# Expert gate by tanh in two vector operations, score banks in groups of three and two, and one shared bank with six turns for each expert tile

## The reference

```python
xn = layernorm(x)
# attention: 16 heads of width 8
q, k, v = (proj(xn, W) * mod for W in (Wq, Wk, Wv))
scores = einsum('bhid,bhjd->bhij', q, k) / sqrt(8) * cos_mat
w = softmax(scores); w = (w + roll(w, 1, axis=-1)) / sqrt(2)
attn = einsum('bhij,bhjd->bhid', w, v) -> (tokens, 128) @ Wo
# experts: 8, two chosen for each token by a small attention over the expert logits
for e in range(8):
    a, g = split(x_rep @ w1[e].T, 2, axis=-1)      # 352 + 352 columns
    he = silu(a) * g @ w2[e].T                     # silu(a) = a / (1 + exp(-a))
out = x + attn + sum over the two chosen experts of score * he
```

## Time and profile before

| | us |
|---|---|
| median of 3 runs (lowest to highest) | 792.3 (790.2 to 797.7) |
| the profiled execution | 797.84 |
| its span, first to last instruction | 796.0 |

### The profile page before, as it was taken

How to read it: one execution, slowest core, us unless ns; L and a number is a source line. 1 busy time by engine, 2 the same in 40 slices (tenths; PEclk the granted TensorE clock), 3 DMA queues, 4 the chain that set the end, 5 groups by cost and what they waited for, 6 DMA issues and landing times.

```text
span 796.0 us, 11999 instructions
## 1 busy us (share of the span) xinstructions
PE 673.1 (85%) x4346; PEld 232.9 (29%) x4346; DVE 367.9 (46%) x648; ACT 534.4 (67%) x535; POOL 77.7 (10%) x91
## 2 busy tenths in 40 slices
PE   3946899798888978887988988987888899999996
PEld 1432132233323323333333333333333111111113
DVE  6652552143466366554464565555646232404002
ACT  2553968766656566655556566566665899999992
POOL 4000077200000000000000000000000245300000
PEclk9965999988989899978899799799999999999998
DMA  8346421441212112121121121121110112000001
GB/s 253 125 149 150 130 77 51 148 137 61 85 68 68 70 54 81 70 74 62 70 65 70 70 75 62 70 86 49 70 38 7 47 37 65 25 1 2 2 1 55
DMA packets 49582, 57.34 MB, mean 72 GB/s; under 512 B 7356, under 2 KB 39126, under 8 KB 49266
## 3 DMA queue, kind: packets, MB, share of 16 engines
q1 hardware_dynamic: 46546, 52.34, 20.5%
q0 software_dynamic: 2048, 4.20, 1.7%
q10 hardware_dynamic: 928, 0.00, 0.1%
HBM read 21.14 MB, written 13.63 MB: 44 GB/s over the span
## 4 chain that ended last, share of the span: by engine, by line
PE 48%; DVE 23%; ACT 12%; issue 11%; SPq 2%; DMA 2%; ACTq 1%; DVEq 0%
PE ps L1165 17%; DVE cs L823 12%; PE ps L1148 11%; ACT big L618 9%; PE ps L1082 5%; PE ps L1091 5%; PE ps L1183 3%; DVE cs L825 3%; DVE cs L828 3%; DVE m L871 2%; ACT cs L611 2%; DVE cs L822 2%; PE ps L986 2%; PE ps L1072 1%; PE ps L1025 1%
## 5 line engine op out<-in xcount | busy, mean ns | idle before, releaser
L618 ACT ACTIVATE big<-ps 128x1024 f32<-128x1024 f32 (+1 forms) x459 | 491.4, 1125 | 217.5 <-PE ps L1148 215.4
L1165 PE MATMUL ps<-big,vh 128*32 128x512 f32 x2048 | 291.8, 644 | 0.4 <-ACT big L618 0.4
L1148 PE MATMUL ps<-qa,ka 49*128 49x512 f16 x896 | 176.2, 404 | 16.6 <-DMA qa<-shift_rows 8.3
L871 DVE TENSOR_REDUCE m<-ps 128x1 f32<-128x512 f32 x128 | 88.4, 690 | 95.3 <-PE ps L1183 95.3
L823 DVE RECIPROCAL cs<-cs 128x384 f32<-128x384 f32 x39 | 99.6, 2553 | 1.4
L1148 PEld LDWEIGHTS ps<-qa,ka 49*128 49x128 f16 x896 | 38.8, 94 | 173.0 <-ACT big L618 101.1
L1091 PE MATMUL ps<-store,cs 128*128 128x128 f32 (+1 forms) x234 | 38.4, 303 | 58.1 <-DVE cs L828 58.0
L1082 PE MATMUL ps<-xgT,store 128*128 128x128 f32 (+1 forms) x468 | 80.0, 312 | 2.7 <-DMA store<-w2T 2.7
L1082 PEld LDWEIGHTS ps<-xgT,store 128*128 128x128 f32 (+1 forms) x468 | 62.1, 199 | 54.7 <-issue 51.7
L1165 PEld LDWEIGHTS ps<-big,vh 128*32 128x32 f32 x2048 | 41.2, 110 | 92.2 <-issue 81.1
L1183 PE MATMUL ps<-ka,attnT 49*128 49x512 f16 x128 | 51.5, 402 | 11.1 <-DVE m L871 11.1
(11 more groups left out here) (160 smaller groups left out, 333.3 us busy)
## 6 DMA issues: line engine op xcount, KB each, us to landing
store<-w1T SPq DMA_DIRECT2D x39, 352.0 KB, 2.6
store<-w2T SPq DMA_DIRECT2D x39, 192.0 KB, 2.5
qk_parts<-store SPq DMA_DIRECT2D x16, 256.0 KB
qa<-qk_parts SPq DMA_DIRECT2D x28, 128.0 KB
slots_x<-vh SPq DMA_DIRECT2D x5, 512.0 KB, 6.4
cs<-slots_x SPq DMA_DIRECT2D x20, 128.0 KB, 2.3
slots_y<-y SPq DMA_DIRECT2D x19, 128.0 KB, 1.8
ka<-qk_parts SPq DMA_DIRECT2D x32, 64.0 KB, 2.0
```

The lines of the kernel that those rows point to most:

```text
L618: nc.scalar.activation(probs[:, prob_of(tiles[0]):prob_of(tiles[-1]) + 1, :], ps[:, bank_of(tiles[0]):bank_of(tiles[-1]) + 1, :], ACT.Exp, ...
L871: nc.vector.tensor_reduce(m4[:, j // NC, j % NC:j % NC + 1], ps[:, O_BANKS[(p - 1) % 2], :], AX, ALU.max).then_inc(m_reduced, 1)
L1148: ins = nc.tensor.matmul(ps[:, bank_of(n), :], k[at:at + KQ, P * o:P * o + P], q[at:at + KQ, CW * c:CW * c + CW], start=True, stop=True, t ...
L1165: ins = nc.tensor.matmul(ps[32 * c:32 * c + 32, O_BANKS[p % 2], :], vh[:, p % 2, o + 8 * b, :], probs[:, prob_of(n), :], start=k == 0, sto ...
```

## The change

- The gate uses silu(a) = 0.5 a (1 + tanh(a / 2)). ScalarE computes tanh(a / 2) with the function Tanh. VectorE then does two `scalar_tensor_tensor` operations with PSUM: (t + 1) times a (`take_a`), and 0.5 times that times g (`take_g`). The add, the clamp and the reciprocal are gone.
- All 1024 score tiles go in groups of three and two in turns, over a ring of five banks (0 to 4) and fifteen SBUF slots: 410 groups.
- Bank 5 (`SIDE_BANK`) is shared by the weight transposes, the rows, a, g and the result. So g is made after a has been taken (`a_taken`), the next rows after the result has been copied (`y_copied`), and each weight block after the copy of the one before.
- An expert tile takes six turns: rows in 0, a in 1 (with the tanh), g in 3, result in 5. Expert turns run from 56 to 289. VectorE's share of a piece comes at the start of the next turn (`take_a` at the start of step 3's turn), ahead of the max job and the head's work.
- Max jobs start from the fifth quad of a head instead of the seventh, are allowed in every turn, and choose the row half that differs from the half of the group's last score tile.
- SP issues the first rows and staged weights at turn 50 (before: 66), the result store one turn later in a tile; the gather starts at quad 188 (before: 174).

```diff
+LARGE_GROUP, SMALL_GROUP = 3, 2
+RING = LARGE_GROUP + SMALL_GROUP
+PROBS = 3 * RING
+SIDE_BANK = 5
-JOB_QUAD = 6
+JOB_QUAD = 4
-EXPERTS_AT = 70
-TURNS_A_TILE = 7
-GATHER_AT = 174
+EXPERTS_AT = 56
+TURNS_A_TILE = 6
+GATHER_AT = 188
...
         def first_of(g):
-            if g < PAIRS:
-                return 2 * g
-            return min(PAIRED + GROUP_OF * (g - PAIRS), SCORE_TILES)
+            return min(RING * (g // 2) + LARGE_GROUP * (g % 2), SCORE_TILES)
...
-                if (w % QUADS >= JOB_QUAD and j < jobs_before(w // QUADS + 1) and step not in (4, 5)
-                        and (g < PAIRS or (g - j) % 2 == 0)):
-                    job = (w // QUADS, j)
+                if w % QUADS >= JOB_QUAD and j < jobs_before(w // QUADS + 1):
+                    half = (first_of(g) + 1) % 2
...
-                nc.scalar.activation(decay[:, m % 2, :], ps[:, 4, 0:FP], ACT.Exp, scale=-1.0).then_inc(decay_ready, 1)
+                nc.scalar.activation(turned_gate[:, m % 2, :], ps[:, SIDE_BANK, 0:FP], ACT.Tanh, scale=0.5).then_inc(gate_ready, 1)
...
-            def hidden(m):
+            def take_a(m):
                 k = m % 2
-                dve.wait_ge(decay_ready, m + 1)
-                then(nc.vector.tensor_scalar(decay[:, k, :], decay[:, k, :], 1.0, BIGGEST, ALU.add, ALU.min))
-                then(nc.vector.reciprocal(decay[:, k, :], decay[:, k, :]))
+                dve.wait_ge(gate_ready, m + 1)
                 dve.wait_ge(a_ready, m + 1)
-                then(nc.vector.tensor_tensor(decay[:, k, :], decay[:, k, :], ps[:, 4, 0:FP], ALU.mult))
+                nc.vector.scalar_tensor_tensor(turned_gate[:, k, :], turned_gate[:, k, :], 1.0, ps[:, SIDE_BANK, 0:FP],
+                                               ALU.add, ALU.mult).then_inc(a_taken, 1)
+
+            def take_g(m):
+                k = m % 2
                 dve.wait_ge(g_ready, m + 1)
+                dve.wait_ge(a_taken, m + 1)
                 after(dve, y_ready, m - 1)
-                nc.vector.tensor_tensor(hidT[:, k, :, :].rearrange("p f s -> p (f s)"), decay[:, k, :], ps[:, 5, 0:FP],
-                                        ALU.mult).then_inc(hidT_ready, 1)
+                nc.vector.scalar_tensor_tensor(hidT[:, k, :, :].rearrange("p f s -> p (f s)"), turned_gate[:, k, :], 0.5,
+                                               ps[:, SIDE_BANK, 0:FP], ALU.mult, ALU.mult).then_inc(hidT_ready, 1)
...
             for g, job, quads in turns():
+                m, step = expert_step(g)
+                before_m, before_step = expert_step(g - 1)
+                if weight_block(g - 1) is not None:
+                    take_weights(weight_block(g - 1))
+                if before_step == 0:
+                    rows_out(before_m)
+                if step == 3:
+                    take_a(m)
+                if before_step == 3:
+                    take_g(before_m)
+                if before_step == 5:
+                    result_out(before_m)
                 if job is not None:
                     take_max(*job)
...
-                after(pe, wT_ready, i - 1)
+                after(pe, wT_ready, i)
...
+                after(pe, y_copied, m)
+                nc.tensor.transpose(ps[:, SIDE_BANK, FP:FP + P], xg[:, m % 4, :], ident[:]).then_inc(xgT_ps, 1)
...
                 if b == 1:
-                    after(pe, y_copied, m)
+                    pe.wait_ge(a_taken, m + 1)
...
-                after(pe, exp_done, g if g == PAIRS else g - 1)
-                if g == PAIRS:
-                    pe.wait_ge(hidT_ready, TILES)
-                    pe.wait_ge(y_copied, TILES)
+                after(pe, exp_done, g - 1)
```

More of the change, by code:

```diff
@@ L240, in build @@
         xg_ld, y_wr = ([sem(f"{n}{half}") for half in range(2)] for n in ("xg_ld", "y_wr"))
-        xgT_ps, xgT_ready, a_ready, g_ready, decay_ready = (
-            sem(n) for n in ("xgT_ps", "xgT_ready", "a_ready", "g_ready", "decay_ready"))
+        xgT_ps, xgT_ready, a_ready, g_ready, gate_ready, a_taken = (
+            sem(n) for n in ("xgT_ps", "xgT_ready", "a_ready", "g_ready", "gate_ready", "a_taken"))
         hidT_ready, y_ready, y_copied, gather_ld, y_added = (
@@ L301, in groups_for, with job_in @@
         def groups_for(n):
-            if n <= PAIRED:
-                return -(-n // 2)
-            return PAIRS + -(-(n - PAIRED) // GROUP_OF)
+            whole, rest = divmod(n, RING)
+            return 2 * whole + -(-rest // LARGE_GROUP)
         def quads_for(n):
             return (n - 1) // NC + 1
-        def job_at(j):
-            return j // PER_HEAD, j // NC % NT, (2, 0, 3, 1)[j % NC]
+        def job_in(half, k):
+            r, i, c = k // (2 * NT), k // 2 % NT, 2 * half + k % 2
+            return r, i, c
         def jobs_before(p):
@@ L329, in turns @@
         def turns():
-            w, j = 0, 0
+            w, j, taken = 0, 0, [0, 0]
             for g in range(SCORE_GROUPS + 2):
-                m, step = expert_step(g)
                 job = None
-                if (w % QUADS >= JOB_QUAD and j < jobs_before(w // QUADS + 1) and step not in (4, 5)
-                        and (g < PAIRS or (g - j) % 2 == 0)):
-                    job = (w // QUADS, j)
+                if w % QUADS >= JOB_QUAD and j < jobs_before(w // QUADS + 1):
+                    half = (first_of(g) + 1) % 2
+                    if taken[half] == JOBS // 2:
+                        half = 1 - half
+                    job = (w // QUADS, j, *job_in(half, taken[half]))
+                    taken[half] += 1
                     j += 1
@@ L468, in _ @@
                     load_rows(m // 2 + 2)
-                if step == 0 and m % 2 == 0 and m >= 2:
+                if step == 1 and m % 2 == 0 and m >= 2:
                     store_results(m // 2 - 1)
-                if g == EXPERTS_AT + TURNS_A_TILE * TILES:
+                if g == EXPERTS_AT + TURNS_A_TILE * TILES + 1:
                     store_results(ROW_PAIRS - 1)
@@ L616, in weights @@
                 act.wait_ge(score_ready, g + 1)
-                after(act, pv_done, quads_for(held_before(tiles[-1]) + 1))
+                if tiles[-1] >= PROBS:
+                    act.wait_ge(pv_done, quads_for(tiles[-1] - PROBS + 1))
                 nc.scalar.activation(probs[:, prob_of(tiles[0]):prob_of(tiles[-1]) + 1, :],
@@ L636, in _ @@
                 m, step = expert_step(g)
-                if step == 3:
-                    decay_of(m)
+                if step == 1:
+                    gate_of(m)
             project(0)
@@ L805, in take_weights @@
                 dve.wait_ge(tr_ready, i + 1)
-                e, b, bank = i // NF, i % NF, 4 + i % 2
+                e, b, bank = i // NF, i % NF, SIDE_BANK
                 if b < 2:
@@ L1098, in expert_work @@
                     turn_rows(m)
-                elif step == 2:
+                elif step == 1:
                     widen(m, 0, a_ready)
@@ L1102, in expert_work @@
                     widen(m, 1, g_ready)
-                elif step == 6:
+                elif step == 5:
                     result(m)
```

47 lines of the change are left out of this document (13 added, 34 removed).

## The result

| | before | changed |
|---|---|---|
| median time, us | 792.8 (790.2 to 797.7, 4 runs) | 707.2 (706.6 to 708.3, 4 runs) |
| ratio, 95% interval | | 0.8915 [0.887, 0.896] |
| profiled execution, us | 797.8 | 706.55 |
| its span, us | 796.0 | 704.7 |
| mean granted clock of the span | 0.92 | 0.97 |

The forecast was 702 us, range 685 to 732. The measured time is inside, 5 us above the forecast.

A forecast was written before the change was run, and what follows sets the result against it. TensorE's waits for VectorE's gate chain and the clock falls behind them bound the expert stage, ScalarE the last. Stages 66.8 + 39.1 + 39.9 + 7.0 + 386.5 + 145.3 + 16.0 = 700.6, plus 1.8 around: 702 us, range 685 to 732.

The forecast's parts named there:

- Waits cost twice: Expert stage before: 58.0 us of TensorE waits for the gate chain, plus 42 us of full-speed work lost by clock.
- Block prices: Expert turns: TensorE blocks priced from start to next start at clock 1.00, summing to 374.0 us.
- Jobs behind a pair: Expert turns: max jobs needing the maximum before wait in short turns, 3.8 and 2.7 us.
- the first widens: Expert turns: in 20 tiles without a quad in turn 1, the first widen waits for the rows' copy, 3.0 us.
- Weight transposes: Weight stage, 39.9 us: with one bank six turns wait about 0.35, three 0.15, w2 copies 0.6 more: 3.1 us.
- SP's and POOL's queues: SP's rows and weights move ahead of head 3's operands, store and gather move with the tiles: no cost taken.
- The last stage: 299 tiles after the expert turns: 140.2 us of ScalarE, times 1.036, gives 145.3 us.
- The shared bank as a new wait: Two waits a tile for the shared bank in the expert turns, 168 us more, 870 us; chance 0.03.
- Clock staying low: Clock falls persist though the waits are gone, 20 to 40 us stay: 720 to 740; chance 0.10.
- ScalarE as the bound of the expert turns: ScalarE needs 10.3 us a tile with idling: 402 us instead of 386.5, about 718 in all; chance 0.10.
- Table loads: Tanh and Exp share no table: two 1.28 us loads a tile, expert turns 433, total 749 us; chance 0.04.
- The rule on banks: Skill rule set against the forecast: without rotating banks every side-work handover stands open; the row says only short turns.

The follow-up runs named there:

- the last experiment: Changed kernel with seven turns a tile, spaced max jobs, one gather a quad, head 2's values copied before the scatter's second half: 687.3 us, ratio 0.8672.

## Why the prediction was right, and where it was off

| stage | predicted | measured |
|---|---|---|
| up to the first scores | 66.8 | 65.3 |
| turns 0 to 25 | 39.1 | 40.5 |
| weight transposes | 39.9 | 39.0 |
| to the first rows | 7.0 | 11.6 |
| expert turns | 386.5 | 383.2 |
| scores behind them | 145.3 | 149.4 |
| end | 16.0 | 15.7 |
| span | 700.6 | 704.7 |

- **Waits cost twice.** Right, and shown: with nothing but the gate changed the same stage lost 101 us, where 58 of waits and 42 of clock were read from it. Taken off the span, 796.0 - 100, they give about 696 us for a kernel with the gate alone; the nearest run of that kind, which also has one weight bank, had a span of 699.1, of which 4.75 are the bank: 694.4. The working had this number in its hands and did not write it down. So it saw that the change would gain, but not that the rest of it gives back some 8 us (side by side, with the standstill) to 10 (704.7 - 694.4).
- **Block prices.** Right. The blocks priced from starts before summed to 374.0; in the changed kernel they come to 367, with 16 of waits. Jobs behind a pair waited 8.4 instead of 6.5, the first widens 4.5 instead of 3.0. The clock fell once near the stage's start, for 3.4 us at 152.4, still ahead of the first rows, where 3 us of cost had been put inside the stage. So the stage's 386.5 against 383.2 is closer than its parts, blocks 7 too high, waits 6 too low, the fall 3 too high, and that much of it is luck.
- **Weight transposes.** Right. A block behind a pair without a quad starts 0.69 after it instead of 0.32: the wait for the copy, 0.35 as worked out.
- **SP's and POOL's queues.** This is the step that failed: "Nothing for these" was worked out for SP alone. The slots are ready at the same turn as before, but that turn now comes at tile 60 instead of 48, so GpSimd's scatter ends later (its memset starts at 148.17 instead of 142.59), and the copy of head 2's values, which waits for nothing but its turn in the queue, came after TensorE's quad wanted it. It took 11.6 us instead of 7.0; undone, 8.1. The queue explains 3.4 of the 4.6; the other 1.2 stay open.
- **The last stage.** A term mis-sized: ScalarE's 140.2 us times 1.036 for the idling seen before. Measured 149.4, a factor of 1.066. ScalarE was busy for 138.0 us, near the sum, but it stood longer for the scores than it had (changed kernel first, then the one before, each in its last stage):

```profile
ACT big L611 <- PE ps L1146: 11.0, 23, 1.4
ACT big L618 <- PE ps L1148: 6.8, 9, 1.7
```

  TensorE for its part waited 9.4 us for exponentials and 4.3 for maxima there, where it had waited 6.2 and 3.2. That 1.036 came from a stretch in threes almost throughout. That the groups of two among the threes, whose exponential is shorter, bring the extra idling is argued here and not shown: no run changed the last stage alone.
- **Rivals.** The shared bank as a new wait: not here (1.1 us in the expert turns), real with the old gate (4.0 a tile). Clock staying low: no, 1.00 in the expert turns. ScalarE as the bound of the expert turns: no, busy for 298 of 383 us. Table loads: none; with a sigmoid 432 us for the stage.
- **The rule on banks.** The Trainium skill (Perfetto Trace Analysis, Matmuls) advises to rotate independent matmul groups through PSUM banks. By the runs its cost follows the row, not every handover: 4.75 us in 24 blocks, some of whose turns are shorter than block and copy, and in the expert turns 1.1 us, where at least a turn's scores lie between.

## What to carry to other kernels

Price a long vector chain that the tensor engine waits for by its waits and by the clock that falls behind them; here they were 58 and 42 us, and taking the reciprocal and the add out of the chain of each tile gave both back. When a change has several parts, write the forecast for each part alone from the same numbers: the parts that looked free gave back 8 to 10 of 100 us. When a step is moved, follow it through every queue it stands in, and look at what is late behind it: one 0.3 us copy behind a scatter and a memset cost 3.4 us.

## What the runs showed of the hardware

- **A vector operation held by GpSimd's memset.** L836, a `tensor_scalar` on 128x16 in SBUF, took 2.54 us in the changed kernel, and 2.73 in the last experiment; in the kernel before, where it ran after the memset, the same operation took 0.16. The last experiment's timeline:

```profile
149.52 3.51 POOL L536 MEMSET attnT<- 128x4096 f16 x1 [1.31 <-DMA slots_x<-attnT,slot]
...
149.72 0.69 DVE L857 COPY osb<-ps 128x512 f32<-128x512 f32 x1 [3.09 <-PE ps L1168]
...
150.33 2.73 DVE L841 TENSOR_SCALAR top<-top 128x16 f32<-128x16 f32 x1
```

  Both times it ended 0.03 us after the memset did (153.06 and 153.03 here), while a copy out of PSUM under the same memset kept its 0.69. The Trainium skill (SBUF — State Buffer, SBUF: two separate sides) describes this: VectorE in a two-port mode and GpSimd share a port pair that one of them holds for a whole instruction. The times agree with it in two cases; in which mode the operation ran no trace here shows. It cost nothing, since nobody waited.
- **Table loads cost 1.28 us each,** with 0.02 beside them, in 78 of 78. The Trainium skill (ScalarE: Activation LUTs, What ACT_TABLE_LOAD costs) adds a drain of 1.38 to each switch, 2.66 in all. Two such switches would be 5.3 us a tile; ScalarE's own timeline shows 2.6, so here the measurement decides for 1.28.
- **A standstill of 35 to 38 us during an indirect scatter** in one group of runs and not in another, whatever the kernel. TensorE, ScalarE and VectorE idle with no releaser named while GpSimd goes on. Only its place was found, not its cause.
- **A job on the other row half of TensorE is free behind three scores** and costs 0.21 behind a pair, so that the same maximum job has two prices by what stands ahead of it. In the expert turns of the changed kernel the quad starts 0.53 us after three scores without a job (50 times) and 0.54 with one; behind a pair it is 0.32 and 0.54. No run here put the job on the same half.
